# First product started a step earlier, a second pair of hidden banks and another order on VectorE in a graph layer with four experts

## The reference

```python
x = x + _L0_gnn_ref(_layernorm(x, axis=-1), adj, ...)   # 12 heads of 32; scores + adj, softmax, values, Wo
x = x + _L0_ffn_ref(_layernorm(x, axis=-1), ...)

def _L0_ffn_ref(x, router_w, router_b, w1, b1, w2, b2, ln_g, ln_b):
    pooled = x.mean(axis=1)
    logits = pooled @ router_w.T + router_b
    top_v, top_i = jax.lax.top_k(logits, TOP_K)          # 2 of 4 experts for each graph
    gates_k = jax.nn.softmax(top_v, axis=-1)
    gate = jnp.zeros((b, e), x.dtype).at[jnp.arange(b)[:, None], top_i].add(gates_k)
    h = jnp.einsum('bld,edh->belh', x, w1) + b1[None, :, None, :]
    h = jnp.stack([_ACTS[i](h[:, i]) for i in range(e)], axis=1)   # gelu, silu, mish, gelu
    out = jnp.einsum('belh,ehd->beld', h, w2) + b2[None, :, None, :]
    y = jnp.einsum('be,beld->bld', gate, out) + x
    mu = y.mean(axis=-1, keepdims=True)
    var = ((y - mu) ** 2).mean(axis=-1, keepdims=True)
    return (y - mu) * jax.lax.rsqrt(var + LN_EPS) * ln_g + ln_b
```

## Time and profile before

| | us |
|---|---|
| median of 3 runs | 1659.62 (1659.62 to 1659.88) |
| profiled execution | 1659.58 |
| its span | 1657.8 |
| TensorE busy | 1598.8 (96%) |
| VectorE busy | 1179.8 (71%) |
| ScalarE busy | 957.1 (58%) |
| GpSimd busy | 827.4 (50%) |

### The profile page before, as it was taken

How to read it: one execution, slowest core, us unless ns; L and a number is a source line. 1 busy time by engine, 2 the same in 40 slices (tenths; PEclk the granted TensorE clock), 3 DMA queues, 4 the chain that set the end, 5 groups by cost and what they waited for, 6 DMA issues and landing times.

```text
span 1657.8 us, 45212 instructions
## 1 busy us (share of the span) xinstructions
PE 1598.8 (96%) x12756; PEld 1533.7 (93%) x12757; DVE 1179.8 (71%) x3677; ACT 957.1 (58%) x2821; POOL 827.4 (50%) x1235
## 2 busy tenths in 40 slices
PE   8999999999999999859999999999999999999997
PEld 7999999999999999759999999999999999999997
DVE  5888888888888878737755665676677667566764
ACT  6899999999999988832422222333334323243431
POOL 4888888888888877612232333232323223322333
PEclk9999999999999999979999999999999999999999
DMA  6444443355555533872222222222221222222220
GB/s 194 144 141 140 133 141 128 136 173 171 179 178 172 175 127 124 293 292 63 63 73 72 71 72 72 72 72 72 72 72 57 64 71 70 72 72 72 72 69 33
DMA packets 93743, 188.19 MB, mean 114 GB/s; under 512 B 10336, under 2 KB 57440, under 8 KB 91872
## 3 DMA queue, kind: packets, MB, share of 16 engines
q1 hardware_dynamic: 91520, 169.39, 31.3%
q10 hardware_dynamic: 2016, 16.52, 2.7%
HBM read 108.80 MB, written 77.07 MB: 112 GB/s over the span
## 4 chain that ended last, share of the span: by engine, by line
PE 87%; DVE 5%; issue 3%; ACT 3%; POOL 1%; DMA 1%; DVEq 1%; ACTq 0%; POOLq 0%; SPq 0%
PE bank L423 67%; PE bank L497 5%; PE bank L622 4%; PE bank L450 3%; PE bank L520 3%; PE bank L537 2%; PE bank L529 1%; PE bank L506 1%; DVE half_t L1289 1%; DVE inverse L1296 1%; DVE inverse L1292 1%; ACT inverse L889 1%; ACT at_hi L856 1%; DMA ut_scratch<-ut_out 1%; DVE hid L1184 1%
## 5 line engine op out<-in xcount | busy, mean ns | idle before, releaser
L423 PE MATMUL bank<-w_hi,ut_in 128*128 x1536 | 423.8, 343 | 10.1 <-DVE hid L1184 8.9
L685 ACT ACTIVATE prob<-att,neg_max 128x128 f32<-128x128 f32 x768 | 297.3, 390 | 14.8 <-DVE neg_max L1044 11.2
L423 PEld LDWEIGHTS bank<-w_hi,ut_in 128*128 128x128 f32 x1536 | 281.5, 189 | 15.2 <-issue 15.0
L880 ACT ACTIVATE hid<-hid 128x384 f32<-128x384 f32 x192 | 95.1, 526 | 318.0 <-DVE hid L1184 305.2
L423 PE MATMUL bank<-w_hi,at_hi 128*128 x768 | 258.3, 336 | 5.0 <-DVE at_lo L1261 5.0
L1012 POOL TENSOR_SCALAR rs_z<-mv_z 128x1 f32<-128x1 f32 x64 | 14.7, 230 | 497.0 <-DVE mv_z L1315 450.0
L1261 DVE SCALAR_TENSOR_TENSOR at_lo<-bank,gate_col,at_hi 128x384 fp32r<-128x384 f32 x256 | 146.1, 612 | 162.9 <-ACT at_hi L856 162.9
L423 PE MATMUL bank<-w_lo,ut_in 128*128 x768 | 258.2, 336 | 0.0
L423 PE MATMUL bank<-w_hi,at_lo 128*128 x768 | 257.0, 335 | 0.0
L423 PE MATMUL bank<-w_lo,at_hi 128*128 x768 | 256.6, 334 | 0.0
L856 ACT ACTIVATE at_hi<-bank,gate_col 128x384 fp32r<-128x384 f32 x256 | 134.6, 577 | 170.0 <-PE bank L622 168.2
(11 more groups left out here) (135 smaller groups left out, 3826.5 us busy)
## 6 DMA issues: line engine op xcount, KB each, us to landing
xu_scratch<-xu SPq DMA_DIRECT2D x64, 384.0 KB, 2.3
ut_scratch<-ut_out SPq DMA_DIRECT2D x64, 384.0 KB, 2.7
ut_in<-ut_scratch SPq DMA_DIRECT2D x64, 384.0 KB, 3.0
xz<-xu_scratch SPq DMA_DIRECT2D x64, 384.0 KB, 3.1
x_in<-in_x SPq DMA_DIRECT2D x32, 384.0 KB, 4.9
xu<-in_x SPq DMA_DIRECT2D x32, 384.0 KB, 4.2
out_dram<-xz SPq DMA_DIRECT2D x64, 192.0 KB, 1.9
w_lo<-in_L_ffn_w SPq DMA_DIRECT2D x4, 1152.0 KB, 6.0
```

The source lines that it names most:

```text
L423: last = nc.tensor.matmul(acc, lhs[c][a], rhs[c][b], start=start and n == 0, stop=stop and n == len(terms) - 1)
L685: nc.scalar.activation(prob[g][:, hh, :], att[g][:, head, :], ACT.Exp, bias=neg_max[g][:, head:head + 1], scale=-1.0, accum_out=row_sum[g] ...
L880: nc.scalar.activation(hid[k][:, s], hid[k][:, s], ACT.Gelu).then_inc(a_ready[k], 1)
```

## The change

1. The hidden values of k = 0 stay in banks 0 and 1, those of k = 1 go to banks 7 and 6. A first layer waits for the hidden values of job i-2 (of the same banks) instead of job i-1. Job (0,0) uses banks 7 and 1.
2. The first half (384 of 768 columns) of the first product of job (0,0) stands in step 64 on TensorE, ahead of the o product of graph 62, in bank 7; the second half is in step 65. Its input ut_in[0] is loaded in step 61 instead of 63.
3. ScalarE does the activation of job (0,0) inside step 66, ahead of the last normalisation, and waits for the stores of one xu buffer instead of all.
4. For graphs 62 and 63 VectorE itself rounds the attention output and forms the rest, directly behind the scaling.
5. The w2 scratch is laid out by partition, and w2 is one tile, `w2_both`, over stage 1's tiles in the order in which they come free; eight loads of 512 to 4608 elements a partition take the place of eight of 2304. b1 is loaded two steps earlier, b2 goes to SyncE's queue behind the stores.
6. VectorE's order in stage 2, shown below: the gate copy behind the hidden values, `add_experts` behind `split_act_lo` and with a fourth operation, the centring (z - mean) * gamma; `finish` (z * rs + x1) in the place of `normalise_z`, and the bias last. GpSimd's three operations become one, x1 + ln_b, done for graph b-1.
7. The last job's transposes directly follow those of the job before, into banks 0 and 1, its rounded parts lie in ut_in's place, and the two last second layers follow each other.
8. The loop is 2 laps of 28 graphs instead of 14 of 4. The router's second half is spread over jobs (1,0) to (2,1). TensorE's waits at the end of stage 1 stand where a bank is needed.

```diff
+        hid_ps, at_ps, y_ps = (bank[0:2], (bank[7], bank[6])), bank[2:4], bank[4:6]
...
-            with engine.Fori(1, B // 4 - 1) as i:
-                for m in range(4):
-                    step(i * 4 + m, m, i)
+            with engine.Fori(0, 2) as i:
+                for j in range(B // 2 - 4):
+                    step(i * (B // 2 - 4) + 4 + j, j % 4, i * (B // 8 - 1) + 1 + j // 4)
...
-                if h == B - 1:
+                if h == B - 3:
                     sp.wait_ge(xt_mm, B)
                     sp.wait_ge(ut_stored[0], 16)
                     load_ut(0, 0)
...
-                for s in range(2):
-                    reached(pe, hid_done, 2 * i + s - 1)
+                for s in halves:
+                    reached(pe, hid_done, 2 * i + s - 3)
...
-                if h == B + 1:
+                if h == B:
 
                     pe.wait_ge(routed, 1)
                     pe.wait_ge(w1h_loaded, 16 * E)
                     pe.wait_ge(piece_lo, PIECES)
+                    pe.wait_ge(v_done, B)
+                    first_layer(0, 0, 0, 0, choice(0, 0), (0,))
+                if h == B + 1:
                     pe.wait_ge(pt_act, 2 * B)
-                    first_layer(0, 0, 0, 0, choice(0, 0))
+                    first_layer(0, 0, 0, 0, choice(0, 0), (1,))
...
-            def load_w2(half, e):
-                act.dma_start((w2_lo, w2_hi)[half][:, e].bitcast(F32), w2_dram[half, e]).then_inc(w2_loaded, 16)
+            def load_w2(first, last):
+
+                cols = slice(under[first][0], under[last][1])
+                act.dma_start(w2_both[:].rearrange("p h e c d -> p (h e c d)")[:, cols].bitcast(F32),
+                              w2_dram.rearrange("p h e c d -> p (h e c d)")[:, cols]).then_inc(w2_loaded, 16)
...
+                    act.wait_ge(routed, 1)
+                    for g in range(2):
+                        act.wait_ge(xu_stored[0][g], 16 * (B // 4))
+                    activate(0, 0, choice(0, 0))
...
-            act.wait_ge(routed, 1)
-            for g in range(2):
-                for p in range(2):
-                    act.wait_ge(xu_stored[p][g], 16 * (B // 4))
-                act.wait_ge(ut_stored[g], 16 * (B // 2))
...
+                if n >= B - 2:
+                    dve.wait_ge(ot_done, n + 1)
+                    reached(dve, wo_mm, n - 1)
+                    nc.vector.tensor_copy(flat(ot_hi[g][:]), flat(ot[g][:])).then_inc(ot_hi_done, 1)
+                    dve.wait_ge(ot_hi_done, n + 1)
+                    nc.vector.tensor_tensor(flat(ot_lo[g][:]), flat(ot[g][:]), flat(ot_hi[g][:]).bitcast(F32), ALU.subtract).then_inc(ot_lo_done, 1)
...
+                nc.vector.scalar_tensor_tensor(out=z, in0=z, scalar=mv_z[:, 0:1], in1=lng_wide[:], op0=ALU.subtract, op1=ALU.mult).then_inc(z_centred, 1)
...
-                nc.vector.tensor_scalar(z, z, mv_z[:, 0:1], rs_z[:], ALU.subtract, ALU.mult).then_inc(zn_done, 1)
+                reached_before(dve, x_based, b + 1)
+                nc.vector.scalar_tensor_tensor(out=z, in0=z, scalar=rs_z[:], in1=xz[m][:, 0, :], op0=ALU.mult, op1=ALU.add).then_inc(out_ready, 1)
...
-                    if k == 0 and graph(b, -2):
-                        add_experts(b - 2, (m - 2) % 4)
-                    if graph(b, 0):
                         activate_first(b, k, e)
-                        add_output_bias(b, k, m, lap, e)
...
+                    if k == 0 and graph(b, -2):
+                        add_experts(b - 2, (m - 2) % 4)
                     if graph(b, 0):
                         activate_second(b, k, e)
```

## The result

The changed kernel takes 1682.9 us (median of 4 runs, 1682.42 to 1684.44) against 1659.75 us: the ratio is 1.014, 95% interval 1.0122 to 1.0157. The forecast was 1658.3 us with a range up to 1671, so the time lies 24.6 us above it and outside the range. The profiled execution took 1682.42 us, its span is 1680.6 us, 22.8 more than before.

What follows compares the result with a forecast made beforehand. TensorE was taken as the bound, busy 96% of the span, so only its earlier start or its waits counted. 1659.6 - 19.5 (handover) - 5.1 (tail) + 23.3 (VectorE's order) = 1658.3 us, range 1647 to 1671.

Steps and rivals of the forecast that it cites:

- C, the order on VectorE: Stage 2, VectorE's new order: later hidden values make mish jobs cost more, +23.3 us net, bounds +17 and +33.
- the finish: VectorE's finish operation ahead of the bias and the hidden values of (b,1): 0.5 us, GpSimd's ln_b addition at nothing.
- the transposes at 2.5 us: Single mish job (b,1): transposes wait 2.3 us for mish, 2.5 with a handover, formerly 0.87; +11.4 us over seven jobs.
- The long loop's edge: Rival: the jump back of the 28-graph body costs TensorE about 3 us once, 1661.4 us; chance 0.08.
- The -4.0 for the edge: Gain from fewer laps: VectorE's idle time at a lap edge, exposed behind one mish job, goes; -4.0 us.
- A, the handover: Stage 1 to stage 2: earlier o product, gelu and transposes of the first jobs; -19.5 us, ends -12 and -23.
- The rival on transfers: Handover: larger w2 slices compete with ut_in and residual loads, so A is only -11, 1667 us; chance 0.10.
- The 2.0 us charged for the w2 loads: Handover: w2 loads land at 727.6, no slack before the second layer of job (0,0) at 727.9; +2.0, bounds 0 and 8.
- The move of the half product: Handover: half the first expert product put ahead of the o product of graph 62, in TensorE's idle time; at most 1.7 us.
- B, the tail: End of the kernel: last second layers adjacent, -2.0, and shorter operations before the output, -3.1; together -5.1 us.
- Only waits go: Rival: VectorE's order costs nothing and the 8.9 us of waits on hidden values go, 1626 us; chance 0.08.
- Slower by the clock: Rival: waits of some 3 us at mish jobs halve TensorE's clock, C is +34, 1669 us; chance 0.15.

Runs made afterwards that it cites:

- run 2: Mish branch left out, jobs going through gelu, in the changed kernel (1617.17 us) and in the kernel before (1636.43 us).
- run 1: Also called the order run: changed kernel with VectorE's order put back (expert additions and centring directly behind the hidden values, bias ahead of at_lo); 1632.78 us.
- run 5: Changed kernel with GpSimd's addition of ln_b made to wait for VectorE's finish of the graph before; 1665.46 us.
- run 8: Kernel of run 1 with 14 laps of 4 graphs in place of the long loop; 1627.8 us.
- run 7: Handover variants of run 1: moved half product put back, 1632.82 us; first w2 slice issued one step later, 1631.78 us.
- run 6: Kernel of run 5 with 14 laps of 4 graphs in place of the long loop; 1662.19 us.
- run 3: Kernel before with only the second pair of hidden banks added; 1657.24 us, ratio 0.9979.

## Why the prediction was wrong

The sum was 1659.6 - 19.5 - 5.1 + 23.3; measured in the profiled executions it is 1659.6 - 14.8 - 4.2 + 41.8 = 1682.4. Of the 24 us between the two, 18.4 are in C.

**C, the order on VectorE: right in kind, mis-sized by 18.4 us.** The step that failed is the finish, costed at 0.5 us beside a GpSimd addition put at nothing. That the change pays at mish jobs and hardly anywhere else is shown by run 2, that it is the order by run 1. Four things were missing.
- *The finish was costed at 0.5 us, the row of L1320.* It took 1.21. I had put GpSimd's addition of ln_b at nothing, "GpSimd is idle half the time", and didn't ask what runs beside it: it starts when rs_z is done, and so does the finish. This is the largest term, 14.2 us of excess in run 5. A row that spoke for it was in front of me: the power operation at 0.80 instead of 0.58 beside VectorE. I used it for GpSimd's time alone and not for VectorE's.
- *The wait behind the wait.* I priced the transposes at 2.5 us, which came out at 2.46, and stopped there. That 2.46 is luck: the hidden values came 0.7 later than forecast, at T + 7.2, and the transposes 9.03 us behind them and not 9.65 and a handover, since they start once the first half of the last mish operation is done (1040.17, the two halves run from 1039.47 to 1040.50). With the finish at its own length it is 1.95. Two jobs later the second layer waits for at_lo, and the job is 0.76 to 0.96 too long, since the hidden values of the next (b,1) are late too, its gelu stands ahead of at_hi on ScalarE, and at_lo behind both. With the finish at its own length this is 0.23 to 0.47 (run 5), so most of it is a consequence of the first.
- *The long loop's edge.* I had it as a rival with 0.08 and 3 us. It is 2.0 us of idle TensorE in run 2, 2.5 in the order run, where the lower clock behind it adds 1.7 (run 8), 3.2 with the later slice (run 7) and 3.8 in run 5. In the changed kernel the wait of 3.81 us on the mish of (31,0) covers the same moment. Run 5 against run 6 puts all of the long loop at 5.1 us, clock included. The -4.0 for the edge that goes behind (39,1) came as booked (3.4 us there now, as at the other single ones); but in runs 6 and 8 VectorE doesn't idle at the short laps' edges any more, so it was not the long loop that was needed for it.
- *The clock behind the pairs.* I had it as a bound and a rival and not in the sum. It is some 4 us in the changed kernel, behind two of the pairs and behind (31,0). It does not come on top of the other terms: run 5 gives part of it back with the first term (behind the pair at graph 4) and run 6 the rest with the third, so their prices hold it.

The closing is run 6: first and third taken away, and the lower clock gone with them, 45.4 us of excess against 46.6 forecast. In this agreement the single jobs' too dear 2.5 makes up for the waits behind, which I had left out.

**A, the handover: right where the residual comes in time.** In six of the nine kernels T(2,1) is at 760.6 to 762.3, which is 18 to 20 us less than before, the forecast's 19.5. In the changed kernel's execution a residual load landed late beside weight loads two graphs earlier, in stage 1, and attend(62) was 4.3 us later; which load held it is not shown (run 7). The rival on transfers named this kind of wait, but placed it at the end of the handover; I had looked at when the last slice lands (forecast 727.6, measured 731.2, ahead of S(0,0) at 734.65) and not at what is issued beside the first. The 2.0 us charged for the w2 loads is a term that no run shows: in the order run the last slice landed at 727.83 and S(0,0), at 730.11, did not wait for it. That T(0,1) came at 733.3 there, where 731.1 + 2.0 was forecast, is luck: the input of graph 1 landed 0.7 later than forecast, and the first layer behind that wait began at the lower clock and took 4.8 us instead of 3.2. The move of the half product was put at 1.7 at most and is 0.6.

**B, the tail: -4.2 instead of -5.1.** The last two second layers follow each other without a gap, but end 1.5 us earlier and not 2.0. What follows them is 2.6 us shorter and not 3.1, since GpSimd's first operation (0.65 instead of 0.23) and the finish (0.62 instead of the 0.49 of L1320) are longer than the rows of before:

```profile
1668.26 6.52 PE bank L462 x36
...
1676.27 0.65 POOL rs_z L1074
...
1677.65 0.62 DVE xz L1398
```

**The rivals.** "Only waits go" would have had the 8.9 us on hidden values; run 3 shows 2.9, as the same late VectorE then holds at_lo. "Slower by the clock" had a time nearest to the result, 1669. Its condition came true in part: the clock did fall behind the pairs and at (31,0), for some 4 us, but not behind single mish jobs, which stayed under 3 us, and it is not what the 18.4 us are made of. None of the cases was a term of C that was too small.

**The range** took the bounds of the unknown prices to be 0 and the mean I had. The upper bound for the finish should have been its time beside a GpSimd operation. With 1.2 us there, each of the 16 waits on mish is some 0.7 us longer, 11 us in all (an estimate), and the range would have ended at 1682, still just short of 1682.9.

## What to carry to other kernels

An engine that idles ahead of a wait has room there. In this kernel work put ahead of that wait was free as long as it fitted, the same work behind it moved everything that followed, and the price appeared only at the jobs with the longest chain. Before a chain is costed, ask of each operation of VectorE what GpSimd does in the same microsecond. And when a wait is taken away by another buffer, look at which wait on the same late engine comes next: here at_lo stood 3 us behind the hidden values.

## What the runs showed of the hardware that I had not expected

A VectorE operation with two inputs in SBUF, begun behind a GpSimd operation on full tiles, took 1206 ns instead of 619, and the GpSimd one kept its 1.0 us (run 5). The other way round, a small GpSimd operation (128 x 1) begun beside the centring took a mean of 543 ns, where it took 231 before.

The jump back over a body of 28 graphs left TensorE idle for 2.0 to 3.8 us once; no row of TensorE shows such a wait at the 13 edges of a body of 4 graphs. On VectorE it is otherwise: 13 edges of a body of 4 graphs with 3.0 to 3.8 us each in the kernel before, and none of that size around the changed kernel's code (run 8). The instruction queue moved 123 packets in the changed kernel and 72 before and in the short-lap runs:

```profile
q8 instruction: 123, 2.02, 0.5%
```

(The Trainium skill, "Runtime: NRT & Kernel Launch", section "Instruction fetch mechanics", has a taken branch to a page outside the window fetch it before execution goes on; it gives no duration, and the 2.0 to 3.8 us are this case's. More packets for more code fit that, but no run here shows the fetch itself, and the 72 packets are the same in kernels with and without VectorE's idle time at the edges.)
